# A gated state-space layer on one core: VectorE's order in every step, and the order of the last eight steps

## The reference

```
xn   = layernorm(x)
proj = xn @ in_proj_w                      # gate | x, B, C | dt
xBC  = silu(causal 4-tap conv(x, B, C) + bias)
dt   = softplus(dt + dt_bias);  dA = exp(dt * -exp(A_log))
state_t = state_{t-1} * dA_t + (dt_t * x_t) B_t        # per head
y_t     = C_t . state_t + D * x_t
yn   = y * rsqrt(mean over the group(y*y) + eps) * norm_weight * silu(gate)
s    = yn @ out_proj_w
out  = x + s * silu(xn @ W + bias + low-rank part)
```

## Time and profile before

| | |
|---|---|
| median of three executions | 1809.08 us (1808.38 to 1809.49) |
| the profiled execution | 1808.79 us, span 1807.0 us |
| mean granted clock of PE | 0.994 of full speed |
| busy: PE, PE's weight loads | 1765.0 us (98%), 1423.2 us (79%) |
| busy: DVE, POOL, ACT | 1531.2 (85%), 1150.3 (64%), 822.5 (46%) |

### The profile page before, as it was taken

One profiled execution on the slowest core, in us unless ns is written; L12 is line 12 of the kernel. 1 busy time (PEld: TensorE's weight loads), 2 busy tenths in 40 slices (PEclk: granted clock), 3 DMA queues, 4 the chain that ended last, 5 costly groups with the idle time before them and its releaser, 6 DMA issues.

```text
span 1807.0 us, 30621 instructions
## 1 busy us (share of the span) xinstructions
PE 1765.0 (98%) x11416; PEld 1423.2 (79%) x11416; DVE 1531.2 (85%) x1944; ACT 822.5 (46%) x1859; POOL 1150.3 (64%) x1143
## 2 busy tenths in 40 slices
PE   6999999999999999999999999999999999999987
PEld 4877888888888888888777788888888888888865
DVE  6868888888888888888888988889898888888887
ACT  4554354444435344443534444354444435445344
POOL 5428557574755757475697847658474765847476
PEclk9999999999999999999999999999999999999999
DMA  7533334233333423333574323334232333423224
GB/s 251 160 131 108 106 106 140 84 128 106 105 108 103 140 93 118 105 106 115 178 227 146 122 108 127 106 104 132 80 130 103 121 106 106 140 72 129 96 97 146
DMA packets 113507, 220.77 MB, mean 122 GB/s; under 512 B 10448, under 2 KB 46672, under 8 KB 113360
## 3 DMA queue, kind: packets, MB, share of 16 engines
q1 hardware_dynamic: 112320, 218.66, 36.6%
q10 hardware_dynamic: 1040, 0.16, 0.0%
HBM read 204.63 MB, written 14.16 MB: 121 GB/s over the span
## 4 chain that ended last, share of the span: by engine, by line
PE 83%; DVE 7%; ACT 4%; issue 3%; POOL 2%; DMA 1%; SPq 0%; ACTq 0%; DVEq 0%; POOLq 0%
PE ps_conv L1240 9%; PE ps_conv L1243 8%; PE ps_y L1404 6%; PE ps_conv L1246 6%; PE ps_out L1240 6%; PE ps_out L1243 6%; PE ps_gate L1240 6%; PE ps_gate L1243 6%; PE ps_y L1409 5%; PE ps_s L1441 5%; PE ps_out L1246 4%; PE ps_gate L1246 4%; PE turned_x L1326 3%; PE ps_conv L1247 2%; DVE xc L862 2%
## 5 line engine op out<-in xcount | busy, mean ns | idle before, releaser
L862 DVE SCALAR_TENSOR_TENSOR xc<-ps_conv,convw_sb,xc 128x511 f32<-128x511 f32 (+2 forms) x576 | 430.3, 747 | 157.4 <-ACT xc L630 143.9
L1173 POOL TENSOR_TENSOR rstd_col<-mean_square,half 128x1 f32<-128x1 f32 x128 | 92.4, 722 | 529.4 <-ACT mean_square L771 529.4
L955 DVE TENSOR_TENSOR_SCAN decay<-decay,eye 128x1024 f32<-128x1024 f32 x125 | 294.3, 2354 | 1.0 <-DMA decay<-decays_d 1.0
L1160 POOL TENSOR_TENSOR cpre<-cpre,xc 128x1024 f32<-128x1024 f32 x112 | 269.5, 2406 | 0.0
L636 ACT ACTIVATE xc<-xc 128x512 f32<-128x512 f32 x192 | 121.0, 632 | 324.1 <-DVE xc L862 322.8
L1240 PE MATMUL ps_conv<-xn_hi,wconv_hi 128*128 128x512 f32 x768 | 241.9, 437 | 0.0
L1243 PE MATMUL ps_conv<-xn_hi,wconv_lo 128*128 128x512 f32 x768 | 207.4, 392 | 0.0
L1404 PE MATMUL ps_y<-decay,dtx 128*64 128x128 f32 x1984 | 191.9, 280 | 6.2 <-DVE decay L966 5.4
L780 ACT ACTIVATE square<-ps_y 128x512 f32<-128x512 f32 x126 | 75.5, 599 | 230.7 <-DVE ps_y L1004 230.7
L1240 PEld LDWEIGHTS ps_conv<-xn_hi,wconv_hi 128*128 128x128 f32 x768 | 141.4, 194 | 49.3 <-issue 27.2
L1409 PE MATMUL ps_y<-cpre,state 128*64 128x128 f32 x1760 | 172.1, 274 | 0.0
(11 more groups left out here) (230 smaller groups left out, 3857.6 us busy)
## 6 DMA issues: line engine op xcount, KB each, us to landing
decay<-decays_d SPq DMA_DIRECT2D x125, 512.0 KB, 5.4
cpre<-rows_d SPq DMA_DIRECT2D x112, 512.0 KB, 3.9
stage<-w_in_t SPq DMA_DIRECT2D x32, 1024.0 KB, 6.4
stage<-w_out_t SPq DMA_DIRECT2D x16, 1024.0 KB, 5.5
stage<-w_in_t SPq DMA_DIRECT2D x32, 256.0 KB, 3.2
out_sum<-hidden SPq DMA_DIRECT2D x16, 256.0 KB, 5.8
ffn_d<-sgate SPq DMA_DIRECT2D x16, 256.0 KB, 2.2
out<-out_sum SPq DMA_DIRECT2D x16, 256.0 KB, 3.1
```

Of the source, the lines that this page charges most:

```text
L862: e.scalar_tensor_tensor(acc[:, d:], ps[:, 0:BLK - d], convw_sb[:, tile, TAPS - 1 - d:TAPS - d], acc[:, d:], ALU.mult, ALU.add).then_inc(S ...
L955: e.tensor_tensor_scan(d, d, eye8[:, :, :].rearrange("p h i -> p (h i)"), 0.0, ALU.mult, ALU.add).then_inc(scanned(i)[0], 1)
L1160: e.tensor_tensor(cpre[k % 2][:, :, :], cpre[k % 2][:, :, :], xc[i // CPB % 2][:, XT + 1, block_cols(i % NCH)].unsqueeze(1).to_broadcast([ ...
```

## The change

DVE's loop is put into another order: the new state ahead of y, M between y and the gate's product, and the early taps at the end of the step. In the last eight steps (instead of four) ACT makes dtx and xw; each `last` of a step is made with its scan, in a room of its own for the scans that are made ahead; the scan of N-2 moves from step TAIL-1 to TAIL+1; for the chunks 11 to 13 of the finish, the last sum and the final products are made in the PSUM bank, which PE has to wait for; and POOL's cpre stands behind the power in all steps. `...` marks what is left out.

```diff
+SCALED_DTX = N - 8
+SCALED_XW = N - 8
...
+def in_place(f):
+    return on_vector(f) and f < TOK - 2
...
-        last = sb("last", [P, GH, 1])
+        last = [sb(f"last{i}", [P, GH, 1]) for i in range(3)]
...
-                if TAIL <= i < N:
+                if SCALED_DTX <= i < N:
...
-                if TAIL <= i < N - 1:
+                if SCALED_XW <= i < N - 1:
                     w.wait_ge(S["mm_t"], i + 1)
-                    w.wait_ge(S["last"], inner(i))
+                    w.wait_ge(*lasts(i))
...
+            def fin_in_place(u, f):
+                acc = out_sum[:, f % NCH, :]
+                w.wait_ge(S["osum"], u - NCH + 1)
+                e.scalar_tensor_tensor(ps_out[:, :], ps_out[:, :], rstd_col[:, u % 2:u % 2 + 1], acc, ALU.mult,
+                                       ALU.add).then_inc(S["osum"], 1)
+
+            def fin_rest(u, f):
+                acc = out_sum[:, f % NCH, :]
+                factor, addend, _ = last_rooms(f)
+                w.wait_ge(S["osum"], u + 1)
+                w.wait_ge(S["ffn_act"], f + 1)
+                e.tensor_tensor(ps_out[:, :], ps_out[:, :], factor, ALU.mult).then_inc(S["fin1"], 1)
+                w.wait_ge(S["fin1"], f + 1)
+                w.wait_ge(S["fin2"], f)
+                e.tensor_tensor(acc, ps_out[:, :], addend, ALU.add).then_inc(S["fin2"], 1)
...
             def scan(i):
...
+                if i % NCH < NCH - 1:
+                    w.wait_ge(*scanned(i))
+                    w.wait_ge(S["xw"], inner(i) - 1 if i <= TAIL else 0)
+                    if i in AHEAD:
+                        w.wait_ge(landed_prefix[i % NCH], 32)
+                    e.tensor_tensor(last_room(i)[:, :, :], by_head(d)[:, :, P - 1:P], step_sizes(i).unsqueeze(2),
+                                    ALU.mult).then_inc(lasts(i)[0], 1)
...
-                    if i < TAIL:
+                    if i < SCALED_DTX:
...
-                if 0 <= m < N:
-                    w.wait_ge(S["mm_in"], m + 1)
-                    w.wait_ge(S["skip"], m + 1)
-                    e.tensor_tensor(y_bank(m)[:, :], y_bank(m)[:, :], skip[:, :], ALU.add).then_inc(S["y"], 1)
                 if 0 <= m < N and cm < NCH - 1:
                     new = state[(group(m) + cm) % 2]
...
                 if 0 <= m < N:
+                    w.wait_ge(S["mm_in"], m + 1)
+                    w.wait_ge(S["skip"], m + 1)
+                    e.tensor_tensor(y_bank(m)[:, :], y_bank(m)[:, :], skip[:, :], ALU.add).then_inc(S["y"], 1)
+                if i < N:
+                    mixing_matrix(i)
+                if 0 <= m < N:
                     w.wait_ge(S["square"], m + 1)
...
-                if TAIL < i < N:
-                    mixing_matrix(i)
...
+                    elif finished(i) is not None and in_place(finished(i)):
+                        fin_in_place(u, finished(i))
...
-                for k in {TAIL - 4: (N - 1,), TAIL - 2: (N - 3,), TAIL - 1: (N - 2,)}.get(i, ()):
-                    scan(k)
+                f = finished(i)
+                if f is not None and in_place(f):
+                    fin_rest(u, f)
+                if u == N - 2:
+                    fin(f, u + 1)
                 if i < N and conv_early(i) is not None:
                     taps(conv_early(i))
-                if i <= TAIL:
-                    mixing_matrix(i)
-                f = finished(i)
-                if f is not None and on_vector(f) and f < TOK - 1:
-                    fin(f, u + 1)
+                for k in {TAIL - 4: (N - 1,), TAIL - 2: (N - 3,), TAIL + 1: (N - 2,)}.get(i, ()):
+                    scan(k)
...
-                if TAIL < i < N:
-                    left_of_state(i)
...
-                if i <= TAIL and i % NCH > 0:
+                if i < N and i % NCH > 0:
                     left_of_state(i)
...
+                f = finished(u + DRAIN - 1)
+                if f is not None and in_place(f):
+                    w.wait_ge(S["fin2"], f + 1)
```

More of the change, by code:

```diff
@@ L231, in build @@
             mm_conv tap0 tail edge_in edge_sum taps silu
-            landed_decay0 landed_decay1 landed_decay2 landed_ahead0 landed_ahead1 landed_ahead2 scan_ahead
+            landed_decay0 landed_decay1 landed_decay2 landed_ahead0 landed_ahead1 landed_ahead2 scan_ahead last_ahead
             landed_rows0 landed_rows1 st_rows10 st_rows11 st_rows00 st_rows01
@@ L293, in decay_room, with last_room, lasts @@
             return decay[i % 3][:, :]
+        def last_room(i):
+            return last[AHEAD.index(i)] if i in AHEAD else last[0]
         def decays_landed(i):
             return (landed_ahead[AHEAD.index(i)], 16) if i in AHEAD else (landed_decay[i % 3], 16 * (i // 3 + 1))
+        def lasts(i):
+            return (S["last_ahead"], AHEAD.index(i)) if i in AHEAD else (S["last"], inner(i))
         def scanned(i):
@@ L786, in _ @@
                         e.activation(xw[:, h * HD:(h + 1) * HD], turned_x[:, h * HD:(h + 1) * HD], ACT.Copy,
-                                     scale=last[:, h, 0:1])
+                                     scale=last_room(i)[:, h, 0:1])
                     e.activation(xw[:, (GH - 1) * HD:], turned_x[:, (GH - 1) * HD:], ACT.Copy,
-                                 scale=last[:, GH - 1, 0:1]).then_inc(S["xw"], 1)
+                                 scale=last_room(i)[:, GH - 1, 0:1]).then_inc(S["xw"], 1)
                 if i < N and conv_early(i) is not None:
@@ L949, in fin, with step_sizes @@
                 e.tensor_tensor(acc, acc, addend, ALU.add).then_inc(S["fin2"], 1)
+            def fin_in_place(u, f):
[12 more added lines that the diff above has]
+                e.tensor_tensor(acc, ps_out[:, :], addend, ALU.add).then_inc(S["fin2"], 1)
+            def step_sizes(i):
+                g = group(i) % GROUPS
+                return prefix_dt[:, i % NCH, HEADS + g * GH:HEADS + (g + 1) * GH]
             def scan(i):
@@ L964, in mixing_matrix @@
                     w.wait_ge(S["b_tok"], inner(i))
-                w.wait_ge(S["last"], inner(i))
+                if i < N - 1:
+                    w.wait_ge(*lasts(i))
+                else:
+                    w.wait_ge(S["last"], inner(TAIL))
                 e.tensor_tensor(by_head(d), by_head(d), ps_g[:, P:2 * P].unsqueeze(1).to_broadcast([P, GH, P]),
@@ L975, in _ @@
                     b, c, g = batch(i), i % NCH, group(i) % GROUPS
-                    dx, d = dtx[i % 2], decay_room(i)
-                    step_size = prefix_dt[:, c, HEADS + g * GH:HEADS + (g + 1) * GH]
+                    dx, step_size = dtx[i % 2], step_sizes(i)
                     if b == 0:
@@ L989, in _ @@
                         scan(i)
[L990 to L995, removed]
+                    if c < NCH - 1 and i < SCALED_XW:
                         w.wait_ge(S["last"], inner(i))
@@ L999, in _ @@
                         e.tensor_tensor(by_head(xw[:, :]), by_head(turned_x[:, :]),
-                                        last[:, :, :].to_broadcast([P, GH, HD]), ALU.mult).then_inc(S["xw"], 1)
-                if 0 <= m < N:
-                    w.wait_ge(S["mm_in"], m + 1)
-                    w.wait_ge(S["skip"], m + 1)
-                    e.tensor_tensor(y_bank(m)[:, :], y_bank(m)[:, :], skip[:, :], ALU.add).then_inc(S["y"], 1)
+                                        last[0][:, :, :].to_broadcast([P, GH, HD]), ALU.mult).then_inc(S["xw"], 1)
                 if 0 <= m < N and cm < NCH - 1:
```

## The result

The changed kernel takes 1821.45 us (median of four, 1820.91 to 1822.46), the one before beside it 1808.73 (1808.18 to 1809.49): a ratio of 1.0072, with a 95% interval of 1.006 to 1.0085. That is 12.7 us slower, where 1809.0 and at most 1814 had been forecast. The profiled execution took 1821.21 us with a span of 1819.4; PE's granted clock was 0.996, DVE was busy for 1498.7 us.

A forecast was written before the change was run, and what follows sets the result against it. PE was taken to set the time of nearly all steps. The terms 0.8 + 1.8 - 2.7 = -0.1 on 1808.79, with 0.3 up to the median, gave 1809.0; own range 1805.5 to 1812, with rivals 1801 to 1814.

The forecast's parts named there:

- The steady steps: Steps between batch starts and the end: cost nothing, a push of 1.05 at ynt_hi being covered by 1.27 of slack.
- M lies beside ACT's work and costs nothing: Inside a step: M, between y and the gate's product, runs beside ACT's square and tap, so adds no time.
- y's push: Inside a step: the state ahead of y makes y 0.60 later, passed on to ynt_hi, early taps and silu.
- If nothing else became late: Condition for gaining 0.60 at each of 136.65 and 997.24, and 0.54 and 0.98 at the waits for M.
- The first steps, +0.8: Start of the run: PE's product 1.4 late for ynt_hi, 0.54 of waiting for M gone; net 0.8 us slower.
- The second batch, +1.8: Start of the second batch: PE's product 2.8 late, 0.98 of waiting for M gone; net 1.8 us slower.
- The last eight, -2.7: Last eight steps: shorter PE waits for M and xw bring the end 2.7 us sooner; bounds 0 and -8.
- (c): Last eight: final products in PSUM free the port from POOL, the end gives 5.7, so 1806.0; chance 0.1.
- (b): Fourth step of each group: product into ps_out waits 0.4 for ynt_hi, 15 times, 6.0 us, so 1815.0; chance 0.15.
- (a): Both batch starts and the end: PE's waits just go, 8.6 us together, so 1800.5; chance 0.25.

The follow-up runs named there:

- y_first: Changed kernel with y ahead of the new state as before in all steps but the last eight, M staying moved; ratio 1.0048 to the kernel before.
- tail_fin: Kernel before with the new last eight, DVE scaling dtx and xw until N-5, and final products in SBUF as before; 1805.14 us, ratio 0.9984.
- splits: Changed kernel with POOL's four conv-weight differences put ahead of the power in every group's fourth step; 1806.68 us, ratio 0.9994 to the kernel before.
- tail_only: Changed kernel with the old order of y, state and M in all steps but the last eight; ratio 0.9987 to the kernel before.
- state_first: Changed kernel with M behind the early taps as before in all steps but the last eight, state still ahead of y; ratio 1.0091.

## Why the prediction was wrong

**The steady steps, costed at nothing: the step that failed.** "I cost the steady steps at nothing, covered by these 0.2 us of slack alone." The chain that I followed was right: ynt_hi of the step in question ends at 1658.81 and PE's product starts at 1659.20, so the slack is 0.24 where I had worked out 0.2, and no wait of PE for ynt_hi stands in a steady group. But it was one chain of two. The other consequence of the same push, a scan 0.43 later, I didn't carry to POOL. Its power waits for that scan, and behind the power POOL is full for 8.2 us up to square_sum, which PE takes 2.0 us after ps_y has begun. So the term that failed is this zero: it measured 14 times 0.96, 13.4 us, and through POOL's queue and the scan, not through ynt_hi. The trace of the kernel before had the rows for it, and the one thing to ask was what POOL has queued in a group's fourth step and how far its last piece is from the next scan: 0.13 us.

**The rule that I had, used in one place only.** I cited the port pair for the last eight, where rows showed it, and not for the steady steps. The trace gives it there as well: a POOL instruction that starts behind a scan ends its own time less 0.2 behind it (0.25 for a sum of 0.46, 0.35 for a power of 0.54), and one that starts ahead of it lengthens the scan (2.28 to 2.47, or to 3.05). The Trainium skill (SBUF — State Buffer, section SBUF: two separate sides) says that, where a DVE operation has both inputs in SBUF and the POOL operation reads SBUF, the one of the two that starts first keeps the pair for its whole instruction; the scan and square_sum are such a pair, and square_sum's 1.25 beside half a scan and 2.32 beside a whole one agree.

**M lies beside ACT's work and costs nothing: half right.** M did no harm to the gate's product, which starts 1.72 behind y (1.73 forecast). But with M gone from the end of the step DVE comes to the next scan sooner when y's push isn't there, and y_first shows what that costs: 0.65 a group. "If nothing else became late" was the condition to check, and "earlier" belonged in it: a scan that is early holds POOL up just as well.

**The first steps, +0.8:** +0.85 from chunk 0 to chunk 3. PE gains 0.57 at 135.62 (0.60 forecast), gives it up in a wait of 1.58 for ynt_hi at 168.32 as forecast, and the wait for M behind it is gone.

**The second batch, +1.8:** +1.7 from chunk 62 to 67, partly by luck. Less the 7.12 of chunk 62, PE's product into ps_out starts 2.64 late (1023.12 against 1013.36), where I had 2.8. But only 1.8 of that arises in its own step. The rest is a wait of 0.96 for out_sum at 966.92, which I didn't foresee and which costs 1.20, a gain of 0.81 where the wait of 0.85 for the copied state at 981.43 goes, and 0.46 lost at the ps_s of 997.24, where PE now waits 1.29 instead of 0.83.

**The last eight, -2.7:** -3.1. The wait of 3.25 for M is gone (-2.9 at chunk 123; ps_y starts at 1756.5 less the 15.5 of the steps before, forecast 1756.4), the one for xw is 3.39 instead of 4.54 and, less the same 15.5, runs from 1778.0 to 1781.4, where I had 1778 to 1782. ACT's longer queue makes PE wait 1.20 at ps_s of step N-7, and ps_y of chunk 121 is 0.7 later for it, where I had 0.8. The rival (c) overrated the port here: `tail_fin` shows about half a microsecond for the final products.

**Rivals.** (b) had the right kind of event, a small wait once in each group, at the wrong instruction, for the wrong engine, and at 0.4 instead of 0.95. Its condition, a push of 1.27 or more at ynt_hi, did not hold (the push is 1.03). (a) fails with the waits for ynt_hi at 168.32 and 1023.12.

## What to carry to other kernels

Where two engines exclude each other, being first matters more than being quick: follow a push of a few tenths into the other engine's queue, down to the last small instruction that the bounding engine needs, and note by how much each pair is apart before the change. An engine at 64% of the span can be without a gap for 8 us in each group; its idle time was in front of the same step, and moving work into it (`splits`) made the new order harmless. Test a reorder's parts alone: here the gain was in the last eight, and the version that keeps the old order elsewhere, with DVE scaling until N-5, takes 1804.51, 3.9 us less than the kernel before and 16.9 less than the change. Its lead over `tail_only` (1805.85) is not settled by the runs.

## What I had not expected of the hardware

A 128x1 power (0.54 alone) took 0.85, 1.28 or, in `state_first`, 1.69 according to where DVE's scan ended, and passed the difference on to 8 us of work behind it without loss. And of a POOL sum of 0.46 and a scan of 2.3, the sum takes 0.46 when it starts 0.13 ahead of the scan and 2.32 when it starts 0.3 to 0.55 behind it. In the first order the instruction behind the sum is held up instead, for about as long, and there it cost PE nothing.
